# Six tiles of the first attention written out ahead of its loop instead of two, with the early loads and splits in another order

## What is computed

```python
rel = ki - w - qi                                   # w = 64
valid = (jnp.abs(rel) <= w) & (abs_k >= 0) & (abs_k < S)
scores = jnp.where(valid, q @ k_win.T, -1e9)
out = softmax(scores) @ v_win
x = x + tanh(g_xattn[0]) * out
...
x = x + tanh(g_ffn[0]) * moe0(layernorm(x))         # 32 experts, top 8
x = x + tanh(g_xattn[1]) * bidaf(layernorm(x), ctx) # second attention
x = x + tanh(g_ffn[1]) * moe1(layernorm(x))         # 8 experts, top 2
```

## Time and profile before

| what | value |
|---|---|
| median of 3 runs | 1089.28 us (1088.44 to 1089.52) |
| span of the profiled execution | 1088.8 us |
| what the median has beside the span | 0.5 us |
| busy share PE, DVE, ACT, POOL | 84%, 64%, 41%, 50% |
| the attention's units | from about 18 us to 250 us |

### The profile page before, as it was taken

The page is one execution under the profiler, slowest core; times in us unless marked ns, Lnnn a source line. Parts: engine busy times, 40 slices in busy tenths (PEclk is TensorE's granted clock), DMA queues, the critical chain, the costliest instruction groups (busy, mean ns, idle before and its releaser), DMA issues.

```text
span 1088.8 us, 20608 instructions
## 1 busy us (share of the span) xinstructions
PE 911.9 (84%) x5524; PEld 711.6 (65%) x5525; DVE 701.8 (64%) x1978; ACT 441.5 (41%) x1031; POOL 546.5 (50%) x581
## 2 busy tenths in 40 slices
PE   3368888887658999999999907889999997998883
PEld 3367777777546888888888504655656564786672
DVE  5669999997796865555555268675857256443334
ACT  4558888893053444434444202022223223232220
POOL 7246655644005755555552677878600001787641
PEclk9769999998668999999999968979999997999997
DMA  8960000003103776676777874343300020466648
GB/s 247 223 122 2 1 0 0 0 2 108 44 1 87 233 221 209 217 221 208 217 185 130 291 238 133 97 141 101 107 1 20 1 77 19 84 110 136 135 67 246
DMA packets 75225, 127.44 MB, mean 117 GB/s; under 512 B 12480, under 2 KB 52032, under 8 KB 75008
## 3 DMA queue, kind: packets, MB, share of 16 engines
q0 software_dynamic: 21264, 48.02, 19.4%
q1 hardware_dynamic: 32240, 57.47, 17.4%
q10 hardware_dynamic: 21632, 20.85, 5.5%
HBM read 80.62 MB, written 36.77 MB: 108 GB/s over the span
## 4 chain that ended last, share of the span: by engine, by line
PE 54%; DVE 21%; DMA 8%; issue 7%; POOL 6%; ACT 2%; SPq 2%; DVEq 0%; ACTq 0%; POOLq 0%
PE bank L917 17%; PE bank L932 9%; PE bank L1622 5%; POOL yg L1199 4%; DVE ptl L621 4%; PE bank L906 4%; DMA sw<-in_w 4%; PE bank L427 2%; PE bank L1522 2%; DVE nmax L613 2%; PE bank L925 2%; DVE hot_hi L1341 2%; PE bank L1557 2%; PE bank L1681 2%; PE bank L1582 2%
## 5 line engine op out<-in xcount | busy, mean ns | idle before, releaser
L1182 POOL DMA_INDIRECT xg<-token_rows,gather_idx x198 | 191.7, 968 | 209.1 <-PE bank L906 86.4
L917 PE MATMUL bank<-sw,xgt 128*128 x948 | 244.9, 381 | 0.4 <-issue 0.4
L917 PEld LDWEIGHTS bank<-sw,xgt 128*128 128x128 f32 x948 | 165.4, 191 | 15.5 <-issue 0.8
L1199 POOL DMA_INDIRECT yg<-slot_rows,slot_of x128 | 142.1, 1110 | 59.9 <-issue 34.7
L1011 ACT ACTIVATE ssil<-bank 128x128 f32<-128x128 f32 x237 | 65.8, 278 | 210.8 <-PE bank L917 210.8
L932 PE MATMUL bank<-sw,sht 128*128 x474 | 145.2, 389 | 0.1
L1103 DVE COPY xgt<-bank 128x256 f32<-128x256 f32 x198 | 83.9, 424 | 85.7 <-PE bank L906 77.2
L1116 DVE COPY sht<-bank 128x128 f32<-128x128 f32 x237 | 69.2, 292 | 107.1 <-PE bank L925 106.6
L549 ACT ACTIVATE prob<-bank,nmax 128x256 f32<-128x256 f32 x256 | 111.7, 511 | 7.1 <-DVE nmax L613 7.1
L427 PE MATMUL bank<-consts,prob 128*128 128x128 f32 x512 | 84.0, 289 | 34.0 <-DVE ptl L621 31.5
L613 DVE TENSOR_REDUCE nmax<-bank 128x2 f32<-128x512 f32 x128 | 87.7, 686 | 17.3 <-PE bank L414 16.8
(11 more groups left out here) (225 smaller groups left out, 1632.2 us busy)
## 6 DMA issues: line engine op xcount, KB each, us to landing
slot_rows<-ysb ACTq DMA_DIRECT2D x79, 256.0 KB, 3.5
sw<-in_w SPq DMA_DIRECT2D x48, 384.0 KB
kst<-khl SPq DMA_DIRECT2D x32, 224.0 KB, 5.3
token_sums<-zeros SPq DMA_DIRECT2D x2, 2176.0 KB, 13.3
token_rows<-xn SPq DMA_DIRECT2D x8, 512.0 KB, 4.2
sums<-token_sums SPq DMA_DIRECT2D x8, 512.0 KB, 7.6
xg<-token_rows,gather_idx POOLq DMA_INDIRECT x198, 3.6
x<-in_x SPq DMA_DIRECT2D x4, 512.0 KB, 6.0
```

What stands on the lines that cost most here:

```text
L917: mm = pe.matmul(bank[2 + k % 2][:, 0:2 * FF], xgt[:, i % 3, c * P:(c + 1) * P], w[:, :, c, :], start=(c == 0), stop=(c == CH - 1))
L1182: nc.gpsimd.indirect_dma_start(xg[:, (first + i) % XG_RING, 0:ROW[L]], None, rows[L], bass.IndirectOffsetOnAxis(gather_idx[:, i:i + 1], 0) ...
L1199: nc.gpsimd.indirect_dma_start(yg[:, t % Y_TILES, j, :], None, ybuf[L], bass.IndirectOffsetOnAxis(slot_of[:, t, j:j + 1], 0)).then_inc(s_y ...
```

## The change

Tiles 0 to 5 are written out, and the loop has two rounds instead of three (tiles 6 to 13). On PE the one wait for everything is cut up: ahead of tile 2 for key piece 1, ahead of tile 4 for value group 1 and all masks, ahead of tile 6 for key piece 2 and all values. On DVE a wait for the statistics of block 1 comes ahead of tile 2, and the one for all of them ahead of tile 6. `EARLY` and the places of the statistics are spread over u0 to u40, POOL's `ln_rsqrt` of blocks 2 and 3 moves from tile 1 to tiles 4 and 5, and SP's list has another order.

```diff
+HEAD_TILES = 6
-            for t in (0, 1):
+            for t in range(HEAD_TILES):          # PE
+                if t == 2:
+                    pe.wait_ge(s_kst[1], 256)
+                if t == 4:
+                    pe.wait_ge(s_vd, 4)
+                    pe.wait_ge(s_band, BATCH)
                 for k in range(PAIRS):
-                    step(t, k, t, False)
-            for piece in (1, 2):
-                pe.wait_ge(s_kst[piece], 256)
+                    step(t, k, t % 2, False)
+            pe.wait_ge(s_kst[2], 256)
             pe.wait_ge(s_vd, 2 * len(VGROUPS))
-            pe.wait_ge(s_band, BATCH)
-            with pe.Fori(0, (TILES - 4) // 4) as i:
+            with pe.Fori(0, (TILES - HEAD_TILES - 2) // 4) as i:
...
-        EARLY = {0: ("v", 0, 1), 2: ("v", 1, 0), 4: ("v", 1, 1), 5: ("v", 2, 0), 7: ("v", 2, 1), 8: ("k", 2, 0),
-                 10: ("v", 3, 0), 12: ("v", 3, 1)}
+        EARLY = {0: ("v", 0, 1), 9: ("v", 1, 0), 12: ("v", 1, 1), 17: ("k", 2, 0), 21: ("v", 2, 0), 25: ("v", 2, 1),
+                 33: ("v", 3, 0), 37: ("v", 3, 1)}
+        STATS_AT = {4: 1, 28: 2, 40: 3}
...
-                    if isinstance(t, int) and u in (3, 10, 12):
-                        ln_stats(dve, 0, {3: 1, 10: 2, 12: 3}[u])
+                    if isinstance(t, int) and u in STATS_AT:
+                        ln_stats(dve, 0, STATS_AT[u])
...
-            for t in (0, 1):
+            for t in range(HEAD_TILES):          # DVE
+                if t == 2:
+                    dve.wait_ge(s_lnp[0], 4)
...
-                if isinstance(t, int) and t == 1:
-                    ln_rsqrt(pool, 0, 1)
-                    ln_rsqrt(pool, 0, 2)
+                if isinstance(t, int) and t in (1, 4):
+                    ln_rsqrt(pool, 0, {1: 1, 4: 2}[t])
                 if late(t, 1):
                     x_update(t - 1, 1)
-                if isinstance(t, int) and t == 1:
+                if isinstance(t, int) and t == 5:
                     ln_rsqrt(pool, 0, 3)
...
             stack_keys(0)
+            load_x(1)
             load_values(1)
-            load_x(1)
+            stack_keys(1)
+            load_keys(2)
             load_values(2)
-            load_keys(2)
-            stack_keys(1)
             load_x(2)
+            stack_keys(2)
             load_x(3)
             load_values(3)
-            stack_keys(2)
```

More of the change, by code:

```diff
@@ L454, in step @@
                     mm.then_inc(s_pv, 1)
-            for t in (0, 1):
+            for t in range(HEAD_TILES):
[4 more added lines that the diff above has]
+                    pe.wait_ge(s_band, BATCH)
                 for k in range(PAIRS):
-                    step(t, k, t, False)
-            for piece in (1, 2):
-                pe.wait_ge(s_kst[piece], 256)
+                    step(t, k, t % 2, False)
+            pe.wait_ge(s_kst[2], 256)
             pe.wait_ge(s_vd, 2 * len(VGROUPS))
-            pe.wait_ge(s_band, BATCH)
-            with pe.Fori(0, (TILES - 4) // 4) as i:
+            with pe.Fori(0, (TILES - HEAD_TILES - 2) // 4) as i:
                 for j in range(4):
                     for k in range(PAIRS):
-                        step(4 * i + 2 + j, k, j % 2, False)
+                        step(4 * i + HEAD_TILES + j, k, j % 2, False)
             for t in (TILES - 2, TILES - 1):
@@ L557, in step @@
                         k_hi(g)
-            for t in (0, 1):
+            for t in range(HEAD_TILES):
                 for k in range(PAIRS):
-                    step(t, k, t, False)
-            with act.Fori(0, (TILES - 4) // 4) as i:
+                    step(t, k, t % 2, False)
+            with act.Fori(0, (TILES - HEAD_TILES - 2) // 4) as i:
                 for j in range(4):
                     for k in range(PAIRS):
-                        step(4 * i + 2 + j, k, j % 2, False)
+                        step(4 * i + HEAD_TILES + j, k, j % 2, False)
             for t in (TILES - 2, TILES - 1):
@@ L630, in step @@
                         k_lo(g)
-            for t in (0, 1):
+            for t in range(HEAD_TILES):
+                if t == 2:
+                    dve.wait_ge(s_lnp[0], 4)
                 for k in range(PAIRS):
-                    step(t, k, t, False)
+                    step(t, k, t % 2, False)
             dve.wait_ge(s_lnp[0], 2 * BATCH)
-            with dve.Fori(0, (TILES - 4) // 4) as i:
+            with dve.Fori(0, (TILES - HEAD_TILES - 2) // 4) as i:
                 for j in range(4):
                     for k in range(PAIRS):
-                        step(4 * i + 2 + j, k, j % 2, False)
+                        step(4 * i + HEAD_TILES + j, k, j % 2, False)
             for t in (TILES - 2, TILES - 1):
@@ L712, in attention_pool @@
             pool.wait_ge(s_tg, 1)
-            tile(0, 0)
-            tile(1, 1)
-            with pool.Fori(0, (TILES - 4) // 4) as i:
+            for t in range(HEAD_TILES):
+                tile(t, t % 2)
+            with pool.Fori(0, (TILES - HEAD_TILES - 2) // 4) as i:
                 for j in range(4):
-                    tile(4 * i + 2 + j, j % 2)
+                    tile(4 * i + HEAD_TILES + j, j % 2)
             for t in (TILES - 2, TILES - 1):
```

## The result

The changed kernel took 1078.29 us (median of 4 runs, 1074.76 to 1082.96) against 1088.86 (4 runs) for the kernel before in the same comparison: a ratio of 0.9894, 95% interval 0.9863 to 0.9925. It is 10.6 us faster, where 15.3 were predicted. The forecast of 1074.0 missed by 4.3 us, inside its range.

A forecast was written before the change was run, and what follows sets the result against it. DVE's list was taken to bound the attention. Between u8 and u48, 17.2 us of idle go and 3.4 of work come in, u8 is 1.5 earlier: 15.3 us gained, 1089.3 to 1074.0, range 1069 to 1080.5.

The forecast's parts named there:

- What bounds the kernel: Attention: DVE's list is the measure; 19.89 us idle between u8 and u48 can be won.
- Both waits: DVE between u8 and u48: 8.4 us for ACT's `k_hi(2)`, put too early, and 6.9 us for u16's scores.
- a loop's start: Rival, ahead of tile 2: the loop's start, not piece 2, costs the 6 us; time 1079.7; chance 0.08.
- u8 earlier: Tile 0: three half splits leave DVE's list between u3 and u7, bringing u8 1.5 us earlier, at 35.1.
- Piece 1, piece 2, last values in time: u16 to u48: key and value transfers arrive before they are wanted; cost nothing, up to 2 us if transfers run slower.
- The same work later: u8 to u48: moved splits add 3.4 us to DVE, which stays later than ACT; idle there becomes 2.7 us.
- Code fetched in straight tiles: Slower rival, written-out tiles: code queues behind transfers and stops PE 6.6 us each; three stops give 1093.8; chance 0.04.
- The rest of the kernel hands the gain on: Stages behind the attention: the 15.3 us reach the end whole, with 2 us either way.
- two rivals of which neither came: Loop's start costs the 6 us (1079.7, chance 0.08); first stall comes back smaller from late transfers (1077 to 1080, chance 0.15).

The follow-up runs named there:

- the kernel with only the waits: Cut-up waits and six written-out tiles, with loads, splits and statistics as in the kernel before; ratio 0.9959 (0.9933 to 0.9984) to the kernel before.
- the old load order: Changed kernel with SP's list of loads in the old order, splits, statistics and waits staying; ratio 0.9895 (0.9862 to 0.9928) to the kernel before.
- the two waits filled: Changed kernel with idle matmuls in PE's waits of u15 (five) and u20 (three); 1079.23 us, ratio 0.9907 to the kernel before.
- `k_lo` later: Changed kernel with DVE's `k_lo(2)` behind u19 instead of u18, ACT's `k_hi(2)` staying behind u17; ratio 0.9916 (0.9883 to 0.9949) to the kernel before.
- the second comparison: The changed kernel again with nothing edited, ten runs; median 1079.85 us, ratio 0.9913 (0.9886 to 0.9940) to the kernel before.
- the split at 10: Changed kernel with the second half split of value group 1 behind u10 instead of u12; 1075.19 us, ratio 0.9882 to the kernel before.

## Why the prediction was right, and where it was off

**What bounds the kernel.** Right. Both waits were put too early, both went, and DVE's work came out at 72.4 us for 71.9. That a loop's start by itself doesn't hold PE for 6 us was shown by the kernel with only the waits; only a fetch of code behind piece 2's transfers is not excluded.

**u8 earlier.** 1.8 us for 1.5 predicted; between 1.8 and 3.4 over all profiles with the new places.

**Piece 1, piece 2, last values in time.** Right, PE, ACT and DVE have no wait for a transfer of keys or values from u8 to u48. The starts of piece 1 end at 37.79 us, and its last transfers land 5.9 to 6.2 us behind their starts, so by 44.0 (43.8 predicted). PE writes the mask of u16 at 49.60, which leaves 5.6 us for the 5 predicted. With the old load order the last of them takes 8.4 us, and the piece is 0.36 us late.

**The same work later: "DVE stays the later one".** This is the step that failed. The term is the idle time from u8 to u48, 5 x 0.46 + 0.4 = 2.7 us, which measured 7.1 in the first profile and 6.1 in the second. I had taken 50 to 60 us of the kernel before as proof that DVE stays the bound at half clock. But those ten microseconds held two statistics and half splits beside few units, and so much extra work hides a slow PE. At u16 and u17 there is none of it, and a unit of PE at 1.2 GHz takes 2.08 us against DVE's 1.2 to 1.7. Nor did I ask what PE does while DVE has its extra work: it waits, 2.5 us ahead of u15's transposes, and the clock falls. The changed kernel took 79.5 and 78.4 us for the five tiles from u8, 4.9 and 3.8 more than the 74.6 predicted. With the two waits filled they took 75.9 us in one profile, at full clock throughout, and 77.5 in another, where the clock fell in tile 3. So of the first profile's 4.9 us the lost clock is 3.6, and the other 1.3 are there at full clock too.

**The clock behind a wait.** PE waited 2.51 us ahead of u15's transposes, and the transposes at 48.35 us took 1.09 us instead of 0.63. The Trainium skill (TensorE: Matmul & The Clock Gate, HAM oscillation) says that a kernel whose PE waits too long between short bursts falls back to half clock each time. It would have told me to look at the waits that the change creates on PE. The trace agrees in kind, though not with "each time": of the six profiles with this wait unfilled the clock fell in five, and in the one with `k_lo` later it held.

**Code fetched in straight tiles.** The rival that ended slower didn't come: no wait of PE's matmuls without a releaser in tiles 2 to 5, and tiles 4 and 5 take 14.54 and 14.33 us with 14.03 and 13.69 of DVE's work.

**The rest of the kernel hands the gain on.** Only on average. I had put 2 us on it; the router stage alone took between 51.5 and 55.6 us in thirteen profiles, without regard to the change. That the time lies inside the range of 1069 to 1080.5 owes something to its width: its upper end was set for two rivals of which neither came, and the ten runs of the second comparison have a median of 1079.85, 0.65 us inside it.

## What to carry to other kernels

A wait is worth moving behind the last unit that doesn't need its data, and the loads behind it have to move together with the work that reads them: here the new loads with the old places cost 20 us, and the new places with the old loads next to nothing. When extra work of one engine is spread over a loop, look at the engine that waits for it, and keep two pieces of extra work from standing one behind the other: with one half split moved by two units, tile 2 was as short in its one profile as with idle matmuls, though no timed run sets either apart from the changed kernel. To judge whether an engine stays the bound, take a stretch with the same mixture of work, not one where extra work hides the other engine.

## What the runs showed of the hardware

- With 2.3 us of filler in PE's wait of 2.51 us the clock stayed at 1.00 through tile 2 in three profiles of three. Left unfilled, the wait ended within 2 us of a fall to 0.50 of the clock, which lasted 3 to 7 us, in five profiles of six.
- Shorter waits go either way. At the wait of 1.67 or 1.68 us ahead of u20's transposes the clock fell in the changed kernel and held in the one with the split at 10. At the one of 1.75 us ahead of tile 3 it held in both profiles of the changed kernel and fell in one of the two profiles with the same fillers.
- The same router code took 51.5 us in one profile and 55.6 in another, in which its matmuls had 0.50 of the clock for longer. Ten runs of one kernel spread over 13 us.
- Starting a load took SP 0.45 to 0.59 us at 19 to 20 us and 1.1 us right behind the 16 transfers of key piece 1, which had themselves taken 17.32 us to start, 1.08 us each.
